# Loading the experts' first rows from another queue, fewer pad scatters, and late weights in parts, in a fused modulated-linear and mixture-of-experts kernel

## The reference

```
def modulated_linear(x, cond, W):
    ys = cond / sqrt(512)
    d = rsqrt((ys * ys) @ (W * W) + 1e-8)
    return ((x * ys[:, None]) @ W) * d[:, None]

def moe(x, cond, ...):
    shared = (silu(x @ w1) * (x @ w3)) @ w2             # hidden width 1024
    s = sigmoid(concat([x, cond]) @ router_W)            # 8 experts
    top2 = top_k(s + router_bias, 2)
    gates = s[top2] / (sum(s[top2]) + 1e-9)
    routed = sum over the 2 chosen e of gate_e * (gelu(x @ W1e[e]) @ W2e[e])
    return (shared + routed) / 3

x = x + modulated_linear(x, cond, W)
x = x + moe(x, cond, ...)
```

## Time and profile before

| | |
|---|---|
| median of 3 runs | 1156.8 us (1154.67 to 1170.54) |
| profiled execution | 1156.24 us, of which the span of the trace is 1154.4 us |
| PE busy | 1075.8 us (93%) |
| DVE, ACT, POOL busy | 479.2, 315.3, 232.6 us |
| granted TensorE clock, mean | 0.977 |

### The profile page before, as it was taken

How to read it: one execution, slowest core, us unless ns; L and a number is a source line. 1 busy time by engine, 2 the same in 40 slices (tenths; PEclk the granted TensorE clock), 3 DMA queues, 4 the chain that set the end, 5 groups by cost and what they waited for, 6 DMA issues and landing times.

```text
span 1154.4 us, 15574 instructions
## 1 busy us (share of the span) xinstructions
PE 1075.8 (93%) x4976; PEld 875.0 (76%) x4977; DVE 479.2 (42%) x759; ACT 315.3 (27%) x488; POOL 232.6 (20%) x253
## 2 busy tenths in 40 slices
PE   7999899999999999999964989999998799999996
PEld 6778787888888888888843868777787587777874
DVE  5554556685333333333201134444443244444442
ACT  4332432323222222222101123333332133333331
POOL 0000000001113343433451001122311122322222
PEclk9999999999999999999986999999998899999999
DMA  4566578778765777776537059854588855546453
GB/s 166 192 201 232 209 247 274 274 256 246 241 235 185 259 258 235 258 253 232 151 128 148 0 184 275 230 104 82 82 235 254 252 122 100 82 82 101 81 83 45
DMA packets 119773, 209.86 MB, mean 182 GB/s; under 512 B 23920, under 2 KB 78320, under 8 KB 108464
## 3 DMA queue, kind: packets, MB, share of 16 engines
q1 hardware_dynamic: 55136, 142.22, 36.8%
q0 software_dynamic: 25440, 48.38, 19.9%
q10 hardware_dynamic: 39168, 18.88, 6.9%
HBM read 111.01 MB, written 98.65 MB: 182 GB/s over the span
## 4 chain that ended last, share of the span: by engine, by line
PE 54%; DMA 32%; issue 5%; DVE 3%; POOL 2%; SPq 2%; ACT 1%; ACTq 0%; POOLq 0%; DVEq 0%
DMA out<-ys,slot 15%; DMA xs_d<-xrow,sadr 11%; PE banks L486 7%; PE banks L488 7%; PE banks L487 7%; PE banks L422 6%; PE banks L423 6%; PE banks L424 5%; PE banks L436 3%; PE banks L437 3%; PE banks L438 3%; DMA we_d<-ehl 2%; PE banks L388 2%; PE banks L390 2%; PE banks L389 2%
## 5 line engine op out<-in xcount | busy, mean ns | idle before, releaser
L422 PE MATMUL banks<-xh,w13h 128*128 128x512 f32 x512 | 199.5, 390 | 1.9 <-DVE w13l L735 1.9
L423 PE MATMUL banks<-xl,w13h 128*128 128x512 f32 x512 | 199.2, 389 | 0.0
L424 PE MATMUL banks<-xh,w13l 128*128 128x512 f32 x512 | 199.2, 389 | 0.0
L1112 POOL DMA_INDIRECT out<-ys,slot x71 | 110.7, 1559 | 425.5 <-DMA out<-ys,slot 273.8
L757 DVE SCALAR_TENSOR_TENSOR gm<-sil,banks 128x512 f32<-128x512 f32 x64 | 43.9, 686 | 270.1 <-ACT sil L579 270.0
L486 PE MATMUL banks<-we,hidth 128*128 x284 | 115.9, 408 | 16.1 <-issue 13.7
L436 PE MATMUL banks<-wmh,gh 128*128 128x512 f32 x256 | 100.9, 394 | 31.2 <-DVE outst L769 29.0
L486 PE MATMUL banks<-we,xgth 128*128 x284 | 118.6, 418 | 7.2 <-issue 6.6
L579 ACT ACTIVATE sil<-banks 128x512 f32<-128x512 f32 x64 | 38.1, 595 | 316.8 <-PE banks L424 273.5
L488 PE MATMUL banks<-we,hidtl 128*128 x284 | 113.4, 399 | 0.0
L487 PE MATMUL banks<-we,hidth 128*128 x284 | 113.1, 398 | 0.0
(11 more groups left out here) (155 smaller groups left out, 1490.9 us busy)
## 6 DMA issues: line engine op xcount, KB each, us to landing
we_d<-ehl SPq DMA_DIRECT2D x32, 1024.0 KB, 6.3
we<-we_d SPq DMA_DIRECT2D x16, 2048.0 KB, 9.2
xg<-xs_d ACTq DMA_DIRECT2D x144, 128.0 KB
eraw<-expert_w SPq DMA_DIRECT2D x32, 512.0 KB, 5.8
xin<-xT SPq DMA_DIRECT2D x8, 1024.0 KB, 6.5
x1t_d<-x1t SPq DMA_DIRECT2D x8, 1024.0 KB, 8.5
xin<-x1t_d SPq DMA_DIRECT2D x8, 1024.0 KB, 9.1
x_d<-x1tok SPq DMA_DIRECT2D x32, 256.0 KB
```

The costliest lines, as they stand in the source:

```text
L422: pe.matmul(ps[hc % 2][:, :], w_hi, xh[:, j, c, :], start=(c == 0), stop=False)
L423: pe.matmul(ps[hc % 2][:, :], w_hi, xl[:, j, c, :], start=False, stop=False)
L424: last = pe.matmul(ps[hc % 2][:, :], w_lo, xh[:, j, c, :], start=False, stop=(c == DC - 1))
L1112: pool.indirect_dma_start(out[:, :], IO(slot[:, t, 0:1], 0), ys[:, t % RING, :], None, compute_op=ALU.add).then_inc(added, 16)
```

## The change

Three edits, in one step. (a) ACT no longer waits for the scatters and no longer issues the first eight row loads. SP does both, ahead of its load of `slot`; it also waits for `x1_turned`. (b) The pads' places come from a list without gaps: 9216 slots less 8192 pairs are exactly 1024 pads, so 8 scatters of 128 rows instead of 16 of which some rows went to a dummy place. DVE's `pad_rows` is written anew for it. (c) The weights of turns 4 to 7 are loaded in 32 parts of 512 KB instead of 8 loads of 2 MB; SP waits for each part before it issues the next.

```diff
+PADS = (SLOTS - K * TOK) // P
-        padr = small("padr", [2 * E], INT32)
+        padr = small("padr", [PADS], INT32)
-        xs_d = nc.dram_tensor("xs_d", [SLOTS + P, ROW], FP32)
+        xs_d = nc.dram_tensor("xs_d", [SLOTS, ROW], FP32)
@@ sync
+            def load_in_parts(i, e, place):
+                for q in range(4):
+                    sp.dma_start(we[:, bass.ds(place, 1), i % 2, q // 2, q % 2].rearrange("p a c n -> p (a c n)").bitcast(FP32),
+                                 we_d[bass.ds(e * 4 + i % 2 * 2 + q // 2, 1), :, q % 2].rearrange("a p n -> p (a n)").bitcast(FP32)).then_inc(we_in[i % HRING], 16)
+                    sp.wait_ge(we_in[i % HRING], 16 + 16 * (q + 1))
+                sp.sem_inc(weights_in, 1)
...
             weight_loaded(0)
-            sp.wait_ge(pad_out, 16 * 2 * E)
+            sp.wait_ge(xl_ready, DC * 2 * NBLK)
+            sp.wait_ge(x1_turned, DC * NBLK)
+            sp.wait_ge(pad_out, 16 * PADS)
             for b in range(XB):
                 sp.wait_ge(xrow_out[b], 16 * (K * NT // XB))
+            for j in range(RING // PAIR):
+                for g in range(P // Q):
+                    sp.dma_start(xg[g * Q:(g + 1) * Q, j * PAIR:(j + 1) * PAIR].rearrange("p t a n -> p (t a) n"),
+                                 xs_d[j * PAIR * P:(j + 1) * PAIR * P, g * P:(g + 1) * P].rearrange("(a r) d -> r a d", r=Q)).then_inc(xg_in[j], 16)
             sp.dma_start(slot[:, :, :], xs_rec).then_inc(slots_in, 16)
...
                 sp.wait_ge(mm2_done, over + 1)
                 for i in (2 * r, 2 * r + 1):
-                    load_weight(i, e, bass.ds(place, 1))
-                    weight_loaded(i)
+                    load_in_parts(i, e, place)
@@ scalar
-            act.wait_ge(xl_ready, DC * 2 * NBLK)
-            act.wait_ge(pad_out, 16 * 2 * E)
-            for b in range(XB):
-                act.wait_ge(xrow_out[b], 16 * (K * NT // XB))
-            load_rows(0, 0, 0)
-            load_rows(PAIR, PAIR, 0)
@@ vector, pad_rows: 13 operations replaced by
+                then(dve.tensor_tensor(begin[:, 0:E], e8[:, 4, :], count, ALU.add))
+                then(dve.tensor_scalar(begin[:, E:E + 1], e8[:, 1, E - 1:E], float(P), None, ALU.mult))
+                then(dve.scalar_tensor_tensor(free[:, 1:E + 1], e8[:, 0, :], float(P), count, ALU.mult, ALU.subtract))
+                then(dve.tensor_scalar(free[:, 0:1], begin[:, 0:1], 0.0, None, ALU.mult))
+                for d in (1, 2, 4, 8):
+                    dve.tensor_copy(dst[:, 0:d], src[:, 0:d])
+                    then(dve.tensor_tensor(dst[:, d:E + 1], src[:, d:E + 1], src[:, 0:E + 1 - d], ALU.add))
+                    src, dst = dst, src
...
+                dve.tensor_copy(padr[:, :], dst[:, 0:PADS]).then_inc(pad_done, 1)
@@ gpsimd
-            for g in range(2 * E):
+            for g in range(PADS):
                 if g:
                     pool.wait_ge(pad_out, 16 * g)
                 pool.indirect_dma_start(xs_d[:, :], IO(padr[:, g:g + 1], 0), xrow[:, XB - 1, :], None).then_inc(pad_out, 16)
-            pool.wait_ge(pad_out, 16 * 2 * E)
+            pool.wait_ge(pad_out, 16 * PADS)
```

More of the change, by code:

```diff
@@ L869, in pad_rows @@
             def pad_rows():
[L871 to L882, removed]
@@ L883, in pad_rows @@
-                then(dve.tensor_tensor(begin, begin, upto, ALU.mult))
-                then(dve.tensor_scalar(begin, begin, dummy[:, 0:1], None, ALU.add))
-                dve.tensor_copy(padr[:, :], begin).then_inc(pad_done, 1)
+                begin, free, sums = (pad[:, r, :] for r in range(3))
+                count = row(PING)[:, NT - 1, :]
+                place = row(PONG)[:, 0, 0:PADS]
+                grid = row(PONG).rearrange("p a b -> p (a b)")[:, E:E + PADS * (E + 1)].rearrange("p (g e) -> p g e", e=E + 1)
@@ new lines, in pad_rows @@
+                then(dve.tensor_tensor(begin[:, 0:E], e8[:, 4, :], count, ALU.add))
+                then(dve.tensor_scalar(begin[:, E:E + 1], e8[:, 1, E - 1:E], float(P), None, ALU.mult))
+                then(dve.scalar_tensor_tensor(free[:, 1:E + 1], e8[:, 0, :], float(P), count, ALU.mult, ALU.subtract))
+                then(dve.tensor_scalar(free[:, 0:1], begin[:, 0:1], 0.0, None, ALU.mult))
+                src, dst = free, sums
+                for d in (1, 2, 4, 8):
+                    dve.tensor_copy(dst[:, 0:d], src[:, 0:d])
+                    then(dve.tensor_tensor(dst[:, d:E + 1], src[:, d:E + 1], src[:, 0:E + 1 - d], ALU.add))
+                    src, dst = dst, src
@@ new lines, in pad_rows @@
+                then(dve.tensor_tensor(begin[:, 0:E + 1], begin[:, 0:E + 1], src[:, 0:E + 1], ALU.subtract))
+                then(dve.tensor_copy(place, tid[:, 0:PADS]))
+                then(dve.tensor_tensor(grid, place.unsqueeze(2).to_broadcast([P, PADS, E + 1]),
+                                       src[:, 0:E + 1].unsqueeze(1).to_broadcast([P, PADS, E + 1]), ALU.is_ge))
+                then(dve.tensor_tensor(grid, grid, begin[:, 0:E + 1].unsqueeze(1).to_broadcast([P, PADS, E + 1]), ALU.mult))
@@ L887, in slot_rows @@
+                then(dve.tensor_reduce(dst[:, 0:PADS], grid, AX.X, ALU.max))
+                then(dve.tensor_tensor(dst[:, 0:PADS], dst[:, 0:PADS], place, ALU.add))
+                dve.tensor_copy(padr[:, :], dst[:, 0:PADS]).then_inc(pad_done, 1)
             def slot_rows():
```

## The result

The changed kernel takes 1114.7 us in the median (1110.51 to 1116.92, 4 runs), and the kernel before, with its runs beside it, 1163.67 us (1154.67 to 1171.8, 4 runs): a ratio of 0.9577, 95% interval 0.9481 to 0.9672. It is faster. The profiled execution took 1113.13 us with a span of 1111.3 us, where the forecast, made for the profiled execution of before, was 1112.4.

The account below looks back on a forecast made before the run. PE was taken as the bound, stalled by ACT's wait for row scatters and slowed in stage 3 by scatters beside weight loads. 1156.24 - 29.8 - 14 = 1112.4 us, predicted 1112, range 1105 to 1129.

Parts of the forecast that it names:

- (a): Row loads before stage 3: PE regains 28.1 us of waiting plus 1.7 of slow clock; over 20 us of cover.
- (b): Pad scatters before the row loads: scatters end 2 to 5 us earlier, worth 0 once ACT doesn't wait.
- (c): Late weights in stage 3: 6 to 18 us of 17.6 lost come back, 14 taken; parts take 160 us.
- What bounds the kernel: PE, busy 93% of the span; gains only where it idles or runs at its lower clock: two places.
- The four slow tiles: Stage 3, 880.88 to 923.22 us: four tiles beside 2 MB loads take 42.3 us, 17.6 too many.
- the bound of 5 us: Pad scatters: the most that eight fewer could gain if moving the row loads did nothing.
- the case "half": Stage 3: 16 MB in parts cost scatters half of 32.7 us; 25.6 scatters against 25.9 tiles, nothing lost.
- the 12 us that were free: Stage 3, when late weights start: scatters may fall another 12 us behind before PE stops.
- That the parts bring nothing: Stage 3 rival: scatters fall behind as before, only the moved row loads count; 1126 us, chance 0.14 (nothing or little).
- The slower case: Stage 3 rival: any request in flight holds each scatter at 9.71 us; 77 us lost, 1186 us; chance 0.05.
- That the stall only moves: Start of stage 3 rival: SP loads rows late, DVE waits beyond 646.8 us; 1135 to 1142 us, chance 0.04.
- That PE is freed altogether: Stage 3 rival: all 17.6 us come back; 1109 us, or 1106 if later waits shrink; chance 0.17.

Follow-up runs that it names:

- `e_a`: The kernel before with only the first row loads and their waits moved from ACT to SP: 1129.12 us, ratio 0.9774.
- `after_again`: The unaltered changed kernel, run and profiled once more: median 1112.91 us, ratio 0.9566 to the kernel before.
- `e_ac`: The kernel before with row loads moved to SP and late weights in 512 KB parts, but still 16 pad scatters: 1112.53 us, ratio 0.9624.
- `e_c`: The kernel before with only the late weights in 32 parts of 512 KB: 1142.25 us, ratio 0.9881.
- `v_together`: The changed kernel with each four 512 KB parts issued back to back and one wait behind the fourth: 1127.23 us, ratio 0.973.

## Why the prediction was right, and where it was not

**What bounds the kernel** held. The wait of 28.1 us was ACT's place in the program, and `e_a` alone takes it away. The four slow tiles were the ring behind the scatters.

**(a)** was costed at 29.8 us; the first tile of stage 3 comes 30.1 us earlier (27.3 in `after_again`, 29.9 in `e_a`), and the median of `e_a` is 27.0 lower. The loads start at 609.87 us (forecast 611 to 614), and DVE's first turn at 646.52 (646.8) waits for nothing. Holding the loads back into the 20 us of cover shows no cost, as forecast.

**(b)** was costed at 0 beside (a). `e_ac` bears that out to about 5 us. POOL did run into block 7's store: it issues the load at 573.33 us, with 575 to 578 forecast for the landing, and it stands idle from 551.6 us, not from 541. Without (a) the bound of 5 us was too low, mainly by that landing; 7.3 were measured. The new `pad_rows` has 19 operations, six of them between the quoted last lines, and not 23 and seven; the forecast's sum of 3.5 us goes by 19, and in DVE's timeline it takes 3.4 us (248.34 to 251.77), 0.6 more than before, as forecast. From 250 to 260 us PE is busy throughout.

**(c)** was put at 14 us. By the medians it is worth 13.8 alone and 16.6 beside (a), so its size held. Its terms did not. PE got back the whole 17.6 us and not 14. The parts took 162 us (160 forecast), but the 16 MB cost the scatters 24 x (6.47 - 5.63) = 20.2 us instead of 32.7, and 24 x (6.11 - 5.63) = 11.5 in `after_again`: near or below the case "half" of the two that I had. With that PE and the scatters draw apart by less than the 12 us that were free. And the sum stopped at PE. It asked when the ring stops PE and not where the last scatter stands, and so missed what is paid behind the last tile: 8.2 us in the profiled execution, 7.5 in `e_c`, 2.7 in `after_again`, 1.0 in `e_ac`. In the profiled execution, 29.8 + 14 = 43.8 was forecast for 30.1 + 3.1 + 17.6 + 0.5 - 8.2 = 43.1 measured. The 3.1 us are of the first burst, which cost PE less there than in the execution of before. The total was better than its terms, and that it came within 1 us is luck: the terms of `after_again` add up to 46.1.

**The rule against this part**, the Trainium skill's batching to 1 MiB or more ("DMA: Bandwidth & Descriptors", section "Bandwidth"), agrees with the runs about the transfer: from the first issue to the last, 16 MB take 73 us as 2 MB loads (845.20 to 918.6 us in SP's queue), 100 us as 1 MB and 162 us as 512 KB. The rule says nothing on who else needs the engines, and here `v_together` is quicker than the parts by 75 us of loading and slower by 12 to 14 us in the end. The page's fixed cost of about 2 us, in its section on a DMA's anatomy, is for a DMA issued by GpSimd; these are SP's. The estimates from it, 103 us for the parts and 54 for the 2 MB loads, were too short (162 and 73). By them I had put the loss near 13 us (done again, the sum gives 14); measured were 0 for PE and 2.7 to 8.2 behind it.

**The rivals.** That the parts bring nothing is what `v_together` does, not the change. The slower case, each scatter held at 9.71 us by any request in flight, is refuted by scatters that land in 5.3 us beside parts. That the stall only moves is refuted by DVE's first turn, which waits for nothing at 646.52 us, and by `e_a`. That PE is freed altogether is what PE's tiles show; 1109 us weren't reached in the profiled execution for what is paid behind the last tile.

## What to carry to other kernels

A wait on an in-order engine costs what stands behind it in the program; move it to the queue that has nothing urgent behind it, and then shortening what it waits for brings nothing that could be measured here. Background transfers that share DMA engines with a chain of small dependent ones should be paced by a wait; here 1 MB or less in flight was enough, and making them smaller without the wait brought nothing. When a producer is freed, follow its consumer to the very end: a backlog that never stops the producer is still paid behind its last tile. And a term read from one execution should be read from a second one before it is explained.

## What the runs showed of the hardware that was not expected

- An adding scatter of 128 rows landed in 4.8 us in the quiet, 5.3 beside single 512 KB loads (4.9 to 5.4 in six other runs with such loads), 5.5 beside single 1 MB loads, 8.1 beside four 512 KB in flight and 8.6 beside single 2 MB loads (medians). The step between 1 and 2 MB is not explained, and that between 512 KB and 1 MB is not shown.
- The view of the chain that ended last shows only the last 45 us of the changed kernel as scatters and PE before that, because at 1059 us it takes tile 64's product, written at the same time, for what released scatter 62. The times of the scatters themselves show the backlog from tile 23 on. A releaser in a view is the event nearest in time, and a count by index settles it.
